# A wavelet-conv-median kernel: whole images at the end, other early products, five sums by POOL, and POOL no longer paced by DVE

## The reference, cut to what matters

```python
cA, cH, cV, cD = dwt2(x)                       # Haar bands, 16x16 each
proc = lambda c: batchnorm_relu(einsum('bchw,oc->bohw', c, conv_w), bn_gamma, bn_beta)
rimg0 = idwt2(proc(cA), proc(cH), proc(cV), proc(cD))
...                                            # rimg1: three levels of dwt2 and idwt2 on x, which give x back
rimg = concatenate([rimg0, rimg1], axis=1)     # 256 channels
y = conv3x3(rimg, convW_w, 'SAME') + convW_b
x = batchnorm_relu(y, bnW_gamma, bnW_beta)     # statistics over all images and pixels
x_denoised = median_blur(x, 3)                 # 3x3 median per channel, zero padding
out = x + (einsum('bchw,oc->bohw', x_denoised, W) + b)
```

## Time and profile before

| | |
|---|---|
| time, median of 3 runs | 406.03 us (405.81 to 406.16) |
| the profiled execution | 405.87 us, its span 403.6 us |
| PE busy | 391.7 us (97%) |
| DVE busy | 372.1 us (92%) |
| POOL busy | 216.7 us (54%) |
| ACT busy | 168.5 us (42%) |
| mean granted clock of TensorE | 0.998 of full speed |

### The profile page before, as it was taken

The page is one execution under the profiler, slowest core; times in us unless marked ns, Lnnn a source line. Parts: engine busy times, 40 slices in busy tenths (PEclk is TensorE's granted clock), DMA queues, the critical chain, the costliest instruction groups (busy, mean ns, idle before and its releaser), DMA issues.

```text
span 403.6 us, 3844 instructions
## 1 busy us (share of the span) xinstructions
PE 391.7 (97%) x1202; PEld 223.1 (55%) x1202; DVE 372.1 (92%) x528; ACT 168.5 (42%) x364; POOL 216.7 (54%) x208
## 2 busy tenths in 40 slices
PE   7889999999999999999999999999999999998996
PEld 2334568877544445454545555554546588853432
DVE  3799956999949999999999999999999999999996
ACT  1456756322334624243333333434324322266762
POOL 3999469454633548475664747584743440023332
PEclk9999999999999999999999999999999999999999
DMA  8980010010101010101101010101010100003547
GB/s 298 415 353 2 2 52 1 2 52 0 54 1 52 1 52 2 52 0 52 30 24 52 1 54 1 52 1 52 2 52 9 43 2 1 2 0 132 232 168 300
DMA packets 7794, 26.70 MB, mean 66 GB/s; under 512 B 992, under 2 KB 1248, under 8 KB 7776
## 3 DMA queue, kind: packets, MB, share of 16 engines
q1 hardware_dynamic: 7776, 26.48, 17.3%
HBM read 18.09 MB, written 8.39 MB: 66 GB/s over the span
## 4 chain that ended last, share of the span: by engine, by line
PE 61%; DVE 29%; issue 4%; ACT 3%; POOL 1%; DMA 1%; DVEq 0%; SPq 0%; POOLq 0%; ACTq 0%
PE conv_ps L422 43%; PE conv_ps L437 10%; PE one_ps L404 4%; DVE y L996 3%; PE one_ps L515 2%; PE conv_ps L539 2%; DVE sorted_cols L870 1%; DVE sorted_cols L872 1%; DVE sorted_cols L865 1%; DVE sorted_cols L910 1%; DVE one_ps L920 1%; DVE sorted_cols L916 1%; DVE one_ps L899 1%; DVE z L901 1%; DVE z L742 1%
## 5 line engine op out<-in xcount | busy, mean ns | idle before, releaser
L422 PE MATMUL conv_ps<-ru,wt 128*128 128x512 f32 (+1 forms) x360 | 131.1, 500 | 0.0
L422 PEld LDWEIGHTS conv_ps<-ru,wt 128*128 128x128 f32 x360 | 68.2, 190 | 49.5 <-issue 45.7
L422 PE MATMUL conv_ps<-xu,wt 128*128 128x496 f32 (+3 forms) x240 | 87.4, 500 | 0.0
L652 ACT ACTIVATE y<-conv_ps,sgn 128x512 f32<-128x512 f32 (+1 forms) x40 | 25.5, 638 | 129.9 <-PE conv_ps L422 129.9
L422 PEld LDWEIGHTS conv_ps<-xu,wt 128*128 128x128 f32 x240 | 45.5, 190 | 31.7 <-issue 28.6
L251 POOL TENSOR_TENSOR ru<-z 128x512 f32<-128x512 f32 x14 | 18.1, 1292 | 59.1 <-DVE one_ps L905 59.1
L422 PE MATMUL conv_ps<-ru,v 128*128 128x496 f32 (+3 forms) x120 | 43.8, 500 | 0.5 <-POOL ru L252 0.5
L344 POOL TENSOR_TENSOR ru<-eo 128x512 f32<-128x512 f32 x16 | 17.0, 1062 | 43.7 <-DVE one_ps L863 43.5
L404 PE MATMUL one_ps<-y,w 128*128 128x512 f32 x64 | 31.9, 636 | 4.2 <-DVE z L743 2.4
L609 ACT ACTIVATE z<-z,bn 128x256 f32<-128x256 f32 x64 | 33.0, 590 | 0.4 <-DVE bn L808 0.4
L539 PE MATMUL conv_ps<-z,w 128*128 128x512 f32 x64 | 29.5, 599 | 1.9 <-DVE y L996 1.9
(11 more groups left out here) (141 smaller groups left out, 747.1 us busy)
## 6 DMA issues: line engine op xcount, KB each, us to landing
z<-x SPq DMA_DIRECT2D x16, 512.0 KB, 10.3
raw_place<-x SPq DMA_DIRECT2D x15, 512.0 KB, 3.3
out<-y SPq DMA_DIRECT2D x15, 512.0 KB, 2.6
wt<-w_t SPq DMA_DIRECT2D x2, 576.0 KB, 10.1
ru<-x SPq DMA_DIRECT2D x1, 512.0 KB, 14.0
out<-y SPq DMA_DIRECT2D x2, 256.0 KB, 2.6
w<-w_t SPq DMA_DIRECT2D x2, 64.0 KB, 8.0
vec<-vectors SPq DMA_DIRECT2D x1, 3.0 KB, 8.9
```

The source lines that it names most:

```text
L422: return nc.tensor.matmul(bank(u, b)[:, (r0 - row) * BW:(r1 - row) * BW], taps(half, kx, ky), plane[:, (r0 + dy) * BW:(r1 + dy) * BW], sta ...
L652: S.activation(at(slot(n), row * W + b, [[2, cols]]), src, ACT.Identity, scale=sgn[:, :], accum_out=y_sum[:, part:part + 1]).then_inc(y_ke ...
```

## The change

It alters the tables at the top (which products are early, which images are split, which are halved, whose sum is taken by whom, where in the last medians the batch norm and the finishes stand), the waits of POOL, and how the sum is made for images in SUMMED: ACT copies the product into the median's place in `z` and POOL adds it to the mapped y. The unit matrix is gone. Where a half unit is in a bank that a whole image of PRE takes next, PE writes the rest of the bank with zeros (`fill_bank`). The images 14 and 15 are one unit each; of image 15 only the norm and the corners go by halves.

```diff
-    FILLS = {n: 1 for n in range(10, 16)}
-    PRE = (4, 5)
-    SPLIT = (2, 3) + tuple(range(6, 14))
+    FILLS = {n: 1 for n in range(6, 16)}
+    PRE = (2, 3)
+    SPLIT = tuple(range(4, IMAGES))
...
-    SUMMED = (2, 5, 8, 11)
+    SUMMED = (1, 3, 7, 9, 12)
...
-    BN3_AT, FINISH_AT = 9, (16, 20, 24, 28, 32, 36, 40, 44)
-    HALVED = (0, 1, IMAGES - 2, IMAGES - 1)
+    BN3_AT, FINISH_AT = 11, (15, 17, 19, 21, 23, 25, 27, 29)
+    HALVED = (0, 1)
...
-                if n == 7:
+                if n == 5:
                     sp.dma_start(vec[:, :], vectors).then_inc(vec_in, 16)
-                    for half in (X_HALF, R_HALF):
-                        cols = slice(half * KY * KX * CH, (half + 1) * KY * KX * CH)
-                        sp.dma_start(wt[:, cols], w3_cols[:, cols]).then_inc(w3_in[half], 16)
+                if n in (5, 9):
+                    half = X_HALF if n == 5 else R_HALF
+                    cols = slice(half * KY * KX * CH, (half + 1) * KY * KX * CH)
+                    sp.dma_start(wt[:, cols], w3_cols[:, cols]).then_inc(w3_in[half], 16)
...
-                if n == 9:
+                if n == min(FILLS) - 1:
                     mix_taps(X_HALF, 1).then_inc(x_taps_mixed, 1)
...
                 if n >= 2:
-
-                    pool.wait_ge(rows_read, last_unit(n - 2) + 1)
+                    pool.wait_ge(y_done, 2 * (last_unit(n - 2) + 1))
...
             for n in range(2, IMAGES):
-                if n > 3:
-                    pool.wait_ge(mids_read, last_unit(n - 3) + 1)
                 pool.wait_ge(bands_normed, n + 1)
                 pool.wait_ge(q_done, last_unit(n - 2) + 1)
...
+                if n - 3 in SUMMED:
+                    pool.wait_ge(x1_by_act, SUMMED.index(n - 3) + 1)
+                    pool.wait_ge(mix_kept, SUMMED.index(n - 3) + 1)
+                    G.tensor_tensor(slot(n - 3), slot(n - 3), zslot(n - 3), ALU.add).then_inc(out_by_pool, 1)
...
+            def fill_bank(u, b):
+
+                rest = slice(UNITS[u][2] * BW, BANK)
+                nc.tensor.matmul(bank(u, b)[:, rest], zeros[:, :], at(zeros[:, :], 0, [[0, (BANK - UNITS[u][2] * BW) // CH], [1, CH]]),
+                                 start=False, stop=False, skip_group_check=True)
...
+                    if u + 2 < len(UNITS) and UNITS[u + 2][0] in PRE and UNITS[u][2] < H:
+                        fill_bank(u, b)
...
-                    mm = nc.tensor.matmul(conv_ps[:, k, half], w2[:, :], zslot(n)[:, half], start=True, stop=n in OWN)
-                    if n in SUMMED:
-                        pe.wait_ge(x1_by_act, SUMMED.index(n) + 1)
-                        mm = nc.tensor.matmul(conv_ps[:, k, half], unit[:, :], slot(n)[:, half], start=False, stop=True)
+                    mm = nc.tensor.matmul(conv_ps[:, k, half], w2[:, :], zslot(n)[:, half], start=True, stop=True)
...
-                    S.activation(slot(n - 2), conv_ps[:, n % 2, :], ACT.Identity, bias=cb2).then_inc(out_by_act, 1)
+                    S.activation(zslot(n - 2), conv_ps[:, n % 2, :], ACT.Identity, bias=cb2).then_inc(mix_kept, 1)
...
-            last = len(UNITS) - 1
-            del EARLY[last - 3], EARLY[last - 2]
-            LATE[last - 4], EARLY[last - 3] = last - 1, last
...
-            medians(PIECES[:-3])
+            medians(PIECES[:-2])
```

More of the change, by code:

```diff
@@ L124, in wavelet_conv_median_kernel @@
         zero_cols = at(zeros[:, :], 0, [[0, BANK // CH], [1, CH]])
-        unit = w1
         singles = sb("singles", [CH, 19])
@@ L196, in wavelet_conv_median_kernel @@
         mix_done = sem("mix_done")
-        ones_set = sem("ones_set")
-        unit_made = sem("unit_made")
-        out_by_act = sem("out_by_act")
+        mix_kept = sem("mix_kept")
+        out_by_pool = sem("out_by_pool")
         out_ready = sem("out_ready")
@@ L277, in _ @@
                 if n in SUMMED:
-                    sp.wait_ge(out_by_act, SUMMED.index(n) + 1)
+                    sp.wait_ge(out_by_pool, SUMMED.index(n) + 1)
                 else:
@@ L373, in _ @@
                 make_xu03(n)
[L375 to L378, removed]
             def map_x1(n):
@@ L383, in _, with corners_of_halves @@
             pool.wait_ge(bn3_ready, 1)
-            for b in range(2):
-                pool.wait_ge(half_normed, b + 1)
-                G.memset(at(zslot(0), b * (H - 1) * W, [[W - 1, 2]]), 0.0).then_inc(half_ready, 1)
+            def corners_of_halves(n, count):
+                for b in range(2):
+                    pool.wait_ge(half_normed, count + b)
+                    G.memset(at(zslot(n), b * (H - 1) * W, [[W - 1, 2]]), 0.0).then_inc(half_ready, 1)
+            corners_of_halves(0, 1)
             map_x1(0)
-            for n in range(1, IMAGES):
+            for n in range(1, IMAGES - 1):
                 pool.wait_ge(med_normed, n)
@@ L392, in _ @@
                     map_x1(n)
+                if n - 3 in SUMMED:
+                    pool.wait_ge(x1_by_act, SUMMED.index(n - 3) + 1)
+                    pool.wait_ge(mix_kept, SUMMED.index(n - 3) + 1)
+                    G.tensor_tensor(slot(n - 3), slot(n - 3), zslot(n - 3), ALU.add).then_inc(out_by_pool, 1)
+            map_x1(IMAGES - 1)
+            if IMAGES - 4 in SUMMED:
+                pool.wait_ge(x1_by_act, len(SUMMED))
+                pool.wait_ge(mix_kept, len(SUMMED))
+                G.tensor_tensor(slot(IMAGES - 4), slot(IMAGES - 4), zslot(IMAGES - 4), ALU.add).then_inc(out_by_pool, 1)
+            corners_of_halves(IMAGES - 1, 3)
         @block.tensor
@@ L550, in _ @@
             pe.wait_ge(w2_in, 16)
-            pe.wait_ge(unit_made, 1)
             pe.wait_ge(squares_summed, PARTS_ALL)
@@ L556, in _ @@
                 if n - 2 in SUMMED:
-                    pe.wait_ge(out_by_act, SUMMED.index(n - 2) + 1)
+                    pe.wait_ge(mix_kept, SUMMED.index(n - 2) + 1)
                 else:
@@ L675, in put_early @@
                              ACT.Identity).then_inc(pre_put, 1)
-            round_x(SPLIT[0])
             for u in range(len(UNITS)):
@@ L696, in _ @@
             act.wait_ge(bn3_ready, 1)
[L697 to L700, removed]
             def norm_median(n):
                 act.wait_ge(med_made, n + 1)
+                if n in (0, IMAGES - 1):
+                    for b in range(2):
+                        half = z[:, n, b * BANK:(b + 1) * BANK]
+                        S.activation(half, half, ACT.Relu, bias=shift3[:, :], scale=scale3[:, :]).then_inc(half_normed, 1)
+                    return
                 S.activation(zslot(n), zslot(n), ACT.Relu, bias=shift3[:, :], scale=scale3[:, :]).then_inc(med_normed, 1)
-            for n in range(1, IMAGES):
+            for n in range(IMAGES):
                 norm_median(n)
@@ L1007, in step_and_more @@
                     place.pop(done[0])()
-            medians(PIECES[-3:], step_and_more)
+            medians(PIECES[-2:], step_and_more)
             for instruction in sorted(place):
```

6 lines of the change are left out of this document (3 added, 3 removed).

## The result

The changed kernel takes 432.26 us (431.79 to 432.74, 4 runs), the kernel before 405.92 beside it. The ratio is 1.0657, 95% interval 1.0636 to 1.0678: 26 us slower. Forecast were 431.5 us and slower. The profiled execution took 432.74 with a span of 430.7.

A forecast was written before the change was run, and what follows sets the result against it. PE (97%) and DVE (92%) were nearly full; without the waits DVE becomes the bound. DVE's end at 425.7, plus 3.0 last store, 2.3 around the span and half the placing's shortfall, gave 431.5 us; own range 424 to 438, overall 414 to 440.

The forecast's parts named there:

- The bound and the exclusion: Middle: DVE has 0.83 us slack per image; its two-SBUF-operand instructions and POOL's exclude each other, x_lo (2.4 us) included.
- The period: Middle medians: DVE becomes the bound, 18.4 us of work plus 2.9 of stalls, medians 21.3 us apart.
- the placing: Laying POOL's instructions on DVE's windows image by image; for the kernel before it gives 402.7 for 403.6, 0.9 short.
- The start: First images: early fills gain PE 1.7 us; DVE starts image 0 at 64.6, median 2 at 118.0.
- PE at the end: PE's outputs wait for DVE's odd seed, about 2 us per image; y of the last image near 381.
- The tail: After the middle: medians 14 and 15 take 34.7, batch norm 2.4, finishes 13.2, stalls 3.1, last waits 0.6; DVE ends at 425.7.
- the 0.5 added on top: Half the 0.9 us shortfall of the placing, taking the sum from 431.0 to 431.5 us.
- The stable phase: Rival, 10%: in the middle PE stays the bound, DVE at 19.2 us per median; about 405.4 us, no measurable change.
- the waits cost nothing to lose: Rival, 8%: the held instructions at images 0 and 1 have another cause; about 401.5 us, faster.
- The other parts' terms: Fills 1.7 us sooner on PE; images 14 and 15 1.0 less each; gains and stalls of POOL's sums roughly cancel.
- Heavier collisions: Rival, 5%: port held 0.1 us longer per instruction, six hits per median; about 437 to 442 us.

The follow-up runs named there:

- the runs with memsets: Changed kernel with x_lo set to zero by one POOL memset, 404.41 us, or by three memsets one behind the other, 411.29 us.
- the scalar instruction of 2.9 us above: Changed kernel with x_lo made as x times zero by one POOL instruction that reads SBUF: 417.25 us, ratio 1.0294.
- the memset run: Changed kernel with x_lo set to zero by one POOL memset that only writes: 404.41 us, ratio 0.9965.

## Why the prediction was right, point by point

**The bound and the exclusion.** The step that carried it, that two-operand DVE instructions and POOL's reading instructions shut each other out, was read from two held instructions and their partners at image 0. The run with the waits back and the one with them taken from the kernel before show it as the cause of the whole loss; the runs with memsets show that it is POOL's reading. This is what the Trainium skill says too (SBUF — State Buffer, section "Who interferes with whom": contention is with a GpSimd instruction that reads SBUF, not with one that only writes it), and these traces agree: 0.68 to 0.72 us beside memsets, 1.1 to 1.8 beside reading instructions. Where the Trainium skill (the same page, section "SBUF: two separate sides") has the loser block fully for the whole instruction, the traces agree for subtractions and sums, and not for the scalar instruction of 2.9 us above, which let DVE in after 0.9 to 1.1.

**The period.** Forecast 21.3 us with stalls of 0.5, 1.15, 0.4 and 0.9. Measured 21.31, with 0.45, 1.07, 0.71 and 0.83 in the median shown (the starts 245.42, 246.47 and 248.14, and 256.13, 257.44 and 258.87, less 0.60 each). That the mean agrees to 0.01 is luck: most medians are 21.4 to 21.6 us apart, and two of the nine 20.74 and 20.75, each beginning just after a fall of PE's clock (below), which the placing did not have. Over medians 2 to 12 the stalls come to 31.9 us (370.43 less 117.81 less twelve times 18.39) for the forecast 33.0, most of the difference in median 3, whose 3.9 was 3.1.

**The start.** DVE was to start at 64.6 and median 2 at 118.0; in the trace it is 64.5 and 117.8. PE's products for PRE begin at 43.35 against 45.32 in the kernel before, 2.0 sooner for the forecast 1.7, of which the scatter of that start leaves open how much is the fills.

**PE at the end.** Its last output was to end near 381. PE's timeline, the last outputs' first products and the zero products behind them:

```profile
369.42 4.21 PE L425 MATMUL conv_ps<-xu,wt 128*128 128x512 f32 x6 [6.33 <-DVE conv_ps L843]
...
381.03 6.64 PE L557 MATMUL conv_ps<-zeros 128*128 128x512 bf16 x30
```

It ends at 381.03. The wait of 6.33 before it is the missing pq: PE had nothing else to do until the seed.

**The tail.** DVE was to end at 425.7; it ends at 427.69, 2.0 later. Two errors stand behind that: median 14 was to start at 371.7 and starts at 370.43, 1.3 early, and from there to the end it takes 57.3 us for the forecast 54.0. Timelines of DVE and POOL there:

```profile
382.83 0.19 DVE L972 TENSOR_REDUCE singles<-y_sum 128x1 f32<-128x36 f32 x1 [0.80 <-ACT conv_ps L665]
...
402.38 1.70 DVE L904 TENSOR_TENSOR one_ps<-sorted_cols 128x512 f32<-128x512 f32 x1
...
409.74 2.42 DVE L912 TENSOR_TENSOR one_ps<-sorted_cols 128x512 f32<-128x512 f32 x1
...
423.00 1.28 DVE L1000 SCALAR_TENSOR_TENSOR y<-y,vec,conv_ps 128x1024 f32<-128x1024 f32 x1 [1.54 <-PE conv_ps L550]
425.09 2.60 DVE L1000 SCALAR_TENSOR_TENSOR y<-y,vec,conv_ps 128x1024 f32<-128x1024 f32 x3 [0.81 <-PE conv_ps L550]
```

```profile
400.69 2.83 POOL L389 TENSOR_TENSOR y<-y,z 128x1024 f32<-128x1024 f32 x1
...
409.24 2.36 POOL L389 TENSOR_TENSOR y<-y,z 128x1024 f32<-128x1024 f32 x1
```

The stalls in median 15 are the forecast ones, 3.1 by my placing: L904 1.0 and L912 1.7 longer than 0.69, and 0.3 on L902. With POOL's waits back, median 14 and all behind it take 54.2 us (341.87 to 396.10), as forecast. Of the 3.0 more here, 2.8 are DVE's waits: 0.80 before the batch norm for the last squares, where there was none, and 2.71 instead of 0.67 for PE's products with w2. Both go with a slower PE: the x6 at the start of its last outputs took 4.21 us, after a wait in the middle mostly 2.79, and the last products with w2 took 7.59, with POOL's waits back 5.58:

```profile
419.12 7.59 PE L550 MATMUL conv_ps<-z,w 128*128 128x512 f32 x12 [0.65 <-DVE y L1000]
```

```profile
389.67 5.58 PE L552 MATMUL conv_ps<-z,w 128*128 128x512 f32 x12 [1.47 <-DVE y L1002]
```

The granted clock was 0.81 in the first (420 to 431) and 1.00 in the second (390 to 396). The prediction had no term for PE's clock; see below. The sum came out 1.7 short of the profiled execution (431.0 against 432.74), which the 0.5 added on top made 1.2; the median lies 0.8 over the forecast. So the mechanism was right, and the closeness of the number is in part two errors of opposite sign, 1.3 and 3.3.

**The rivals.** The stable phase exists: it is what the memset run shows, 404.4 for the 405.4 worked out for it, but only with x_lo out of the way. That the waits cost nothing to lose is refuted; its time of 401.5, which is that of the other parts alone, came out at 400.9 with the waits kept. The other parts' terms under it: fills 2.0 in time for 1.7, but not seen at PE's end; first products of images 14 and 15 2.2 for 2.0; sums 0. Heavier collisions did not come: the stalls of medians 2 to 12 are 1.1 us under their forecast.

## What to carry to other kernels

When instructions of two engines shut each other out, read their timelines side by side before taking out a wait between them: a wait without a data reason can be what keeps long instructions of one in the gaps of the other. Count the windows in which the full engine runs such instructions, lay the other engine's instructions over them at the phase they would have without the wait, and look whether the loss per period exceeds the slack (here 2.9 against 0.83 us). A gain on an engine can be gone when another becomes the bound: the same parts were worth 5 us with the waits and nothing without them, and one of them, splitting two more images, gave POOL more with which to hold DVE.

## What the runs showed of the hardware that I had not expected

*An instruction of POOL's that outlasts its hold.* The multiplication by a scalar into an fp32r tile took 2.87 us for 1024 columns, though the mapping of y, also with scalars, over as many columns and into f32, takes 1.26. From the groups by line and form of that experiment's kernel:

```profile
L370 POOL TENSOR_SCALAR y<-y,singles 128x1024 f32<-128x1024 f32 x11 | 13.9, 1262 | 0.0
```

DVE was shut out for only 0.9 to 1.1 us of it. Whether the fp32r result or the constant scalar makes it long was not tried.

*PE's clock fell after some of its waits.* Mean granted clock of the changed kernel is 0.972, of the kernel before 0.998. Stretches of the changed kernel, and the tail of the kernel before (the column after POOL's is the granted clock):

```profile
240.00:250.00 10.00, 8.04 (x21) 3.69 (x20) 10.00 (x10) 2.00 (x4) 8.23 (x5) 1.00 0.15 50
260.00:266.00 6.00, 4.05 (x14) 2.10 (x13) 6.00 (x8) 3.21 (x6) 3.46 (x3) 1.00 0.27 87
266.00:270.00 4.00, 4.00 (x6) 1.70 (x7) 4.00 (x4) 0.00 (x0) 4.00 (x3) 0.57 0.00 0
400.00:431.00 31.00, 21.80 (x42) 7.83 (x40) 24.94 (x22) 15.21 (x15) 18.93 (x21) 0.88 0.60 243
```

```profile
369.00:400.00 31.00, 29.08 (x66) 11.49 (x64) 29.44 (x43) 20.39 (x18) 10.35 (x19) 1.00 0.54 220
```

PE's timeline around it:

```profile
244.43 2.79 PE L425 MATMUL conv_ps<-xu,wt 128*128 128x512 f32 x6 [1.96 <-DVE conv_ps L843]
...
254.24 1.23 PE L440 MATMUL conv_ps<-x_hi,taps_hi 128*128 128x512 f32 x3
...
265.86 4.49 PE L425 MATMUL conv_ps<-xu,wt 128*128 128x512 f32 x6 [1.95 <-DVE conv_ps L843]
```

The waits of 1.96 us at 244.43 and 1.95 at 265.86 are alike, but after the second the granted clock is 0.57 on the mean of 4 us, most of it at the lower of its levels (1.2 instead of 2.4 GHz), and the x6 take 4.49 instead of 2.79. Of the eight such waits of 1.9 to 2.0 us three end so (180.66, 265.86, 351.04) and five do not; what decides it these traces don't say. In the middle it costs nothing: the next outputs come later, and so do POOL's instructions, and that median is 20.75 us instead of 21.43 away from the next. In the tail the clock averages 0.88 against 1.00 in the kernel before (and 1.00 with POOL's waits back), and the products with w2 are on the path: DVE's 2.8 us of further waits in the tail go with it. That compares one trace with one other; no run changed the clock alone.
